# Attention with a feed-forward branch on one core: one PV product cut in two, three PSUM evacuations reordered, and one pair of transfers moved to another queue

## The reference

```python
xn = (x - mean(x)) / sqrt(var(x) + 1e-5)
q, k, v = split_heads(xn @ w_qkv.T + b_qkv)
att = q @ k.T / 4 + bias[head, i - j]          # position bias from cosines and sines
att = softmax(where(causal, att, -inf))
attn = merge_heads(att @ v) @ w_proj.T + b_proj
ffn = bf16(fp8(bf16(xn)) @ fp8(kernel)) + bias_ffn
out = x + attn + ffn
```

## Time and profile before

| | before |
|---|---|
| median of 3 runs | 810.27 us (810.13 to 811.91) |
| profiled execution, its own time | 810.14 us |
| its span, first to last instruction | 808.4 us |
| PE busy | 752.4 us (93%) |
| DVE busy | 624.6 us (77%) |
| ACT busy | 578.6 us (72%) |
| POOL busy | 531.1 us (66%) |
| mean granted TensorE clock | 0.968 |

### The profile page before, as it was taken

How to read it: one execution, slowest core, us unless ns; L and a number is a source line. 1 busy time by engine, 2 the same in 40 slices (tenths; PEclk the granted TensorE clock), 3 DMA queues, 4 the chain that set the end, 5 groups by cost and what they waited for, 6 DMA issues and landing times.

```text
span 808.4 us, 23158 instructions
## 1 busy us (share of the span) xinstructions
PE 752.4 (93%) x6313; PEld 515.3 (64%) x6313; DVE 624.6 (77%) x2395; ACT 578.6 (72%) x1258; POOL 531.1 (66%) x525
## 2 busy tenths in 40 slices
PE   6889999999999999999999999999999999999883
PEld 3556566676666766666676667667676666667552
DVE  3869878887978888787887888798788878888612
ACT  3347868777877868777886777777787777777570
POOL 6435568676666767577666857666676767757570
PEclk8859999999999999999999999999999999999997
DMA  5603333534333253333434243443335334343202
GB/s 172 235 2 140 120 123 114 172 115 151 138 145 136 106 189 119 129 137 145 166 117 149 112 159 112 164 140 145 121 119 179 131 122 138 146 146 114 78 18 86
DMA packets 55612, 106.07 MB, mean 131 GB/s; under 512 B 10528, under 2 KB 30496, under 8 KB 55584
## 3 DMA queue, kind: packets, MB, share of 16 engines
q1 hardware_dynamic: 52680, 102.96, 36.2%
q10 hardware_dynamic: 2904, 2.77, 1.1%
HBM read 18.68 MB, written 8.91 MB: 34 GB/s over the span
## 4 chain that ended last, share of the span: by engine, by line
PE 69%; ACT 7%; DVE 7%; issue 6%; DMA 6%; SPq 3%; ACTq 1%; DVEq 1%; POOL 0%; POOLq 0%
PE misc_a L666 13%; PE misc_a L550 10%; PE misc_b L550 10%; PE scoreT_b L640 8%; PE scoreT_a L640 5%; PE score_a L617 4%; PE score_c L617 4%; DMA x_ring<-in_L_attn_x 4%; PE misc_b L666 3%; SPq L341 3%; ACT probs L925 3%; PE misc_b L601 2%; ACT xnT_hi L821 2%; PE scoreT_c L640 2%; DVE row_max L1003 1%
## 5 line engine op out<-in xcount | busy, mean ns | idle before, releaser
L1201 POOL TENSOR_SCALAR_AFFINE_SELECT probs<-probs 128x512 f32<-128x512 f32 x256 | 161.7, 642 | 231.1 <-ACT probs L925 229.5
L1003 DVE CUSTOM_DVE_ANT_0 score_b<-score_b,causal_mask_q 128x384 f32<-128x384 f32 (+3 forms) x321 | 162.0, 522 | 95.8 <-PE score_b L617 95.6
L1003 DVE CUSTOM_DVE_ANT_0 score_a<-score_a,causal_mask_q 128x512 f32<-128x512 f32 x319 | 174.9, 565 | 6.5 <-PE score_a L617 3.2
L925 ACT ACTIVATE probs<-scoreT_b 128x384 f32<-128x384 f32 (+1 forms) x256 | 134.4, 525 | 63.5 <-PE scoreT_b L640 21.1
L1003 DVE CUSTOM_DVE_ANT_0 score_c<-score_c,causal_mask_q 128x256 f32<-128x256 f32 (+3 forms) x384 | 172.0, 476 | 3.0 <-PE score_c L617 2.8
L925 ACT ACTIVATE probs<-scoreT_a 128x512 f32<-128x512 f32 (+1 forms) x256 | 145.4, 568 | 4.5 <-PE scoreT_a L643 3.7
L1003 DVE DVE_READ_ACCUMULATOR2_ANT row_max<- 128x1 f32 x1024 | 145.6, 142 | 0.0
L925 ACT ACTIVATE probs<-scoreT_c 128x384 f32<-128x384 f32 (+1 forms) x256 | 135.9, 531 | 3.4 <-PE scoreT_c L643 3.0
L666 PE MATMUL misc_a<-probs,v_ones 128*32 128x128 f32 (+3 forms) x1536 | 132.1, 440 | 0.4 <-POOL probs L1201 0.4
L640 PE MATMUL scoreT_b<-stacks 64*128 64x384 f32 (+3 forms) x320 | 120.0, 394 | 5.7 <-ACT probs L925 5.7
L617 PE MATMUL score_b<-stacks 64*128 64x384 f32 (+3 forms) x321 | 118.4, 401 | 1.4 <-DVE row_max L1003 1.4
(11 more groups left out here) (241 smaller groups left out, 1957.3 us busy)
## 6 DMA issues: line engine op xcount, KB each, us to landing
stacks<-qk_parts SPq DMA_DIRECT2D x128, 512.0 KB, 3.9
x_ring<-in_L_attn_x SPq DMA_DIRECT2D x16, 512.0 KB, 3.3
xn<-recips SPq DMA_DIRECT2D x31, 256.0 KB
out<-x_ring SPq DMA_DIRECT2D x15, 512.0 KB, 3.0
attn<-out_T SPq DMA_DIRECT2D x48, 128.0 KB, 2.6
stacks<-neg_max_T SPq DMA_DIRECT2D x128, 4.0 KB
attn<-out_T ACTq DMA_DIRECT2D x16, 128.0 KB, 2.7
low_features<-neg_max_T SPq DMA_DIRECT2D x124, 4.0 KB
```

Source lines behind the costliest of these rows:

```text
L925: A(probs_slot(g, k), STB[(SLOTS * g + k) % 3][:, 0:w], ACT.Exp).then_inc(exp_done, 1)
L1003: last = V.tensor_tensor_reduce(bank, bank, CMQ[:, T - w:T], 1.0, LEAST, ALU.add, ALU.max, MX[:, g % 2, 8 * h + 4 + qt:8 * h + 5 + qt])
L1201: last = GP.affine_select(out=d, in_=d, compare_op=ALU.is_ge, fill=0.0, base=0, pattern=[[0, HU], [1, P]], channel_multiplier=-1)
```

## The change

- Unit 3's PV is cut in two sessions: tile 0 at (0, 0) of the next batch, and tiles 1 to 3 at (0, 3). MT then stands behind the last tile. On ACT, `out_T` comes ahead of `max_T` at (0, 4), and behind it on the others.
- The two transfers of unit 3's result go out on SP's queue, behind `load_max(b, 1)`, and no longer on ACT's (but for the last batch).
- The bf16 copies `XB_evac` wait for `T_lo` and stand at (3, 11) and at (0, 3) of the next batch; they had stood right behind each `XH_evac` at (3, 9) and (3, 10). `T_lo` waits for the high half alone and stands at (3, 9) and (0, 2); it had stood at (3, 10) and (0, 0). The bank of T is free when the bf16 copy is done.
- `invert` moves from (0, 6) to (0, 8). `stats`, `aggregate` and `quant_magic` move to other slots.
- In batch 0 and the setup, the evacuations take the same new order.

```diff
-PV_AT = [(1, 0), (2, 3), (3, 3), (0, 3)]
-PV_REST_AT = {0: (1, 3)}
+PV_AT = [(1, 0), (2, 3), (3, 3), (0, 0)]
+PV_REST_AT = {0: (1, 3), 3: (0, 3)}
...
-XL_AT, FIRST_XL_AT = [(3, 10), (0, 0)], [(0, 3), (0, 3)]
-INVERT_AT, LAST_INVERT_AT = (0, 6), (3, 8)
-STATS_AT, AGGR_AT = [(1, 2), (1, 3), (1, 5), (1, 8)], (1, 9)
-MAGIC_AT = [(2, 0), (2, 1), (2, 2)]
+XB_AT, FIRST_XB_AT = [(3, 11), (0, 3)], (0, 4)
+XL_AT, FIRST_XL_AT = [(3, 9), (0, 2)], [(0, 3), (0, 3)]
+INVERT_AT, LAST_INVERT_AT = (0, 8), (3, 8)
+STATS_AT, AGGR_AT = [(1, 3), (1, 3), (1, 6), (1, 6)], (1, 7)
+MAGIC_AT = [(2, 3), (2, 6), (2, 9)]
...
                 load_max(b, 1)
+                if not first:
+                    regroup(b - 1, 3, False)
...
-                return {"V": (vs_ready, 2 * b + i + 3), "T": (xl_ready, 2 * b + i + 5),
+                return {"V": [(vs_ready, 2 * b + i + 3)], "T": [(xb_ready, 2 * b + i + 5)],
...
-                elif then:
+                elif then and g < 3:
                     job_MT(*then)
...
                 if TT - 1 in tiles:
                     last.then_inc(pv_done, 1)
+                if 0 not in tiles and then and g == 3:
+                    job_MT(*then)
...
             def XB_evac(b, ct):
+                act.wait_ge(xl_ready, 2 * b + ct + 1)
                 A(XB[:, ct, :], misc_of("T", ct)[:, :], ACT.Copy).then_inc(xb_ready, 1)
...
-                if g == 3:
-                    act.wait_ge(ot_ready, 4 * b + 4)
+                if g == 3 and isinstance(b, int) and b == B - 1:
+                    act.wait_ge(ot_ready, 4 * B)
                     send_attn(act, b, 3)
...
                         if k == OUT_AT and not (first and g == 0):
+                            if g == 0:
+                                out_T(pb, pg, False)
                             if not (last and g == 3):
                                 max_T(*((b, g + 1) if g < 3 else (b + 1, 0)))
-                            out_T(pb, pg, first and pg == 0)
+                            if g > 0:
+                                out_T(pb, pg, first and pg == 0)
...
             def T_lo(b, ct):
-                dve.wait_ge(xb_ready, 2 * b + ct + 1)
+                dve.wait_ge(xh_ready, 2 * b + ct + 1)
```

More of the change, by code:

```diff
@@ L528, in _ @@
             mm = nc.tensor.matmul
-            bank_read = [None, None]
+            bank_read = [[], []]
             def done(kind, i, b):
-                return {"V": (vs_ready, 2 * b + i + 3), "T": (xl_ready, 2 * b + i + 5),
-                        "QK": (ql_ready, 4 * b + i + 5), "FF": (y1_ready, 2 * b + i + 1),
-                        "PV": (ot_ready, 4 * b + (i + 1) % G), "PJ": (out_ready, 2 * b + i + 1), "MT": (mts_ready, 4 * b + i + 2)}[kind]
+                return {"V": [(vs_ready, 2 * b + i + 3)], "T": [(xb_ready, 2 * b + i + 5)],
+                        "QK": [(ql_ready, 4 * b + i + 5)], "FF": [(y1_ready, 2 * b + i + 1)],
+                        "PV": [(ot_ready, 4 * b + (i + 1) % G)], "PJ": [(out_ready, 2 * b + i + 1)],
+                        "MT": [(mts_ready, 4 * b + i + 2)]}[kind]
             def misc(kind, i, b):
                 n = MISC_BANK[kind, i]
-                if bank_read[n]:
-                    pe.wait_ge(*bank_read[n])
+                for read in bank_read[n]:
+                    pe.wait_ge(*read)
                 bank_read[n] = done(kind, i, b)
@@ L868, in _ @@
                 XH_evac(0, ct)
+            for ct in range(CT):
                 XB_evac(0, ct)
@@ L930, in body @@
                                 XH_evac(1, i)
-                                XB_evac(1, i)
+                            if first and (g, k) == FIRST_XB_AT:
+                                for i in range(CT):
+                                    XB_evac(1, i)
+                            if (g, k) == XB_AT[1] and not first:
+                                XB_evac(b + 1, 1)
                             for i in due(QK_HI_AT, g, k):
@@ L940, in body @@
                                 XH_evac(b + 2, i)
-                                if i == 0:
-                                    act.wait_ge(xy_ready, b + 1)
-                                XB_evac(b + 2, i)
+                            if (g, k) == XB_AT[0]:
+                                act.wait_ge(xy_ready, b + 1)
+                                XB_evac(b + 2, 0)
                         if not first:
```

## The result

The changed kernel takes 842.25 us (840.23 to 844.54, 4 runs) against 811.09 us (810.13 to 812.26, 4 runs): a ratio of 1.038, interval 1.035 to 1.042. That is slower, as forecast, but by 31 us where 11 were expected, and outside the range. (The table of times further up has three of these four runs of the kernel before.) The profiled execution took 840.23 us with a span of 838.5 us. The granted clock is not the cause: 0.965 over the whole run against 0.968 before, and 1.00 in the steady batch of both.

What follows compares the result with a forecast made beforehand. PE, busy 44.75 of a 46.3 us batch, sets the time. Per batch 1.0 - 0.25 = +0.75 us, 15 times 11.25, less 0.5 in the setup: +10.75, so 821.0 us; range 804.5 to 828.

Steps and rivals of the forecast that it cites:

- part 3: Statistics and rounding on DVE: `quant_magic` in later slots of unit 2 costs 0; moved `stats` wins 0.25 us per batch.
- Part 2: Denominators issued later, on SP, delay DVE's reciprocal; the scores of (1, 0) start 1.0 us late in each batch.
- the faster rival: Denominators are in by 433.55, 0.75 us before the estimate, so nothing is lost: about 804.5 us; chance 0.25.
- the time which ACT wins: ACT drops two issues of 0.56 us each; worth nothing, as PE meets the DVE wait at (1, 0) anyway.
- The rival with the maxima late at (1, 0): Transposed scores of (1, 0) wait for the maxima, half a microsecond more per batch: 828 us; chance 0.05.
- that lateness: Inverses' store and spread some 2.7 us late; POOL uses them some 10 us later, in unit 1: cost 0.
- Part 1: At (0, 2) a 0.63 us exponential wait goes; first PV session waits some 0.8; (0, 4) comes 0.27 late.
- FF's 0.25: Ahead of FF, moving one `stats` wins 0.25 us of PE's 0.4 us wait per batch; bounds 0 and 0.4.
- part 4: Setup: high copies first free most of PE's 0.95 us wait before the first QK; -0.5 us, bounds 0, -0.9.

Runs made afterwards that it cites:

- experiment 1: Changed kernel with the three rounding steps put back at slots 0 to 2 of unit 2: 830.87 us, ratio 1.021 to the kernel before.
- experiment 5: Changed kernel with POOL's bf16 bias addition moved behind the last mask of unit 2, DVE untouched: 830.29 us, ratio 1.021 to the kernel before.
- experiment 6: Kernel before with the rounding steps alone moved to (2, 3), (2, 6) and (2, 9): 823.43 us, ratio 1.014.
- experiment 2: Changed kernel with unit 3's two result transfers ahead of the four maxima transfers on SP: 830.75 us, ratio 1.021 to the kernel before.
- experiment 3: Changed kernel with unit 3's two result transfers back on ACT's queue behind `out_T`: 832.45 us, ratio 1.025 to the kernel before.
- experiment 9: Kernel before with the layer norm's statistics alone moved, as in the change: 808.77 us, ratio 0.997.
- experiment 8: Changed kernel with rounding put back, unit 3's PV in one session, second bf16 copy at (0, 1), its low half at (0, 0): 806.41 us, ratio 0.992.
- experiment 12: Kernel before with SP sending unit 3's result behind the maxima, inversion at (0, 8), and statistics moved: 803.55 us, ratio 0.990.
- experiment 10: Kernel before with unit 3's result sent by SP behind the maxima and the inversion at (0, 8): 806.04 us, ratio 0.993.

## Why the prediction was wrong in size

The direction and its main mechanism held. Its sum was +0.75 us per batch, and +2.0 was measured.

**The step that failed: part 3, "both ways cost 0" for `quant_magic`.** The prediction asked only which slot's slack on DVE the steps would use. It did not ask what POOL does at that moment. Experiments 1, 5 and 6 give the term: +0.75 to +0.77 us per batch, 11 us in all, from a step of 0.69 us stretched to 2.15. The Trainium skill has the rule (SBUF — State Buffer, section "SBUF: two separate sides"): DVE and GpSimd share a pair of ports that is locked for a whole instruction, among others against a DVE instruction with two SBUF inputs, and the one that comes second is blocked. The trace agrees: DVE's instruction ends 0.55 us after POOL's, whether they overlap by 1.6 us or by 0.44. And DVE's result step, with one source in PSUM and one in SBUF, takes its 0.68 us (476.48 to 477.16) within POOL's instruction of 475.10 to 477.48. It is the rule against this change that I should have weighed. The rows for it were in the trace of before: from 402 to 405, where the three steps stood, POOL had instructions on 4 values per partition and a mask; from 405.65 to 408.04 and from 409.79 to 411.94, where they were to go, instructions over 1024 columns.

**Part 2, the way of the denominators: mechanism right, size 1.0 against 1.4.** The links, in us from the batch's start, forecast and found: SP's first maxima transfer 6.64 and 6.80; the denominators' issue 10.09 and 10.56; the reciprocal 12.34 and 12.82; from it to PE's scores 1.31 and 1.23; PE's scores of (1, 0) 13.65 and 14.05, against 12.65 before. From issue to reciprocal it was 2.26 us, where 2.25 was taken. Two links were mis-sized. "The bf16 copy for MT's bank ends a little before that and is hidden behind `out_T`" was wrong: PE waits 0.42 us for it, and `max_T` 0.23 us for MT. And between the fourth maxima issue and the attn issue there were 0.40 us, not 0.13. Experiments 2 and 3 show the cause, by removing the wait in two ways. Four issues again took 2.72 us, and the faster rival, which needed the denominators 0.75 us sooner, falls. That the time which ACT wins is worth nothing against this held: the changed kernel wins 0.4 us from (0, 6) to (0, 9), and loses it again at (1, 0). The rival with the maxima late at (1, 0) came up nowhere. What came up was unit 2's: its four transfers stand behind the spread of the inverses and unit 0's stacks on SP's queue, which the late inversion pushes back, and at (2, 0) PE waited for them in several kernels (in the changed one it comes 0.3 us later from (1, 11) to (2, 0) than before, absorbed by the shorter wait ahead of FF). I had costed that lateness at 0, by looking at POOL's use of the inverses and not at what is queued behind them on SP.

**Part 1: right in its wait, short in its end.** The wait for the first bf16 copy was forecast at 0.8 and found at 0.86 on average (0.81 in this batch); the wait for the exponential went. Slot (0, 4) came 0.73 us late where 0.27 was worked out; the difference is MT's wait, named above, here for PE itself.

**Part 3, FF, and part 4.** FF's 0.25 was found as 0.2 in the changed kernel and 0.2 alone (experiment 9); the setup's 0.5 was found as 0.5.

**The sum with what was measured:** 1.4 - 0.2 + 0.75 = 1.95 per batch, 15 times 29 us, near the measured 31. The range missed for the same reason: the term costed at nothing had no upper bound. Its upper end, +1.2 per batch, is just what the other parts came to (1.4 - 0.2). With 11 us for the missing term, 828 would have been 839; the profiled execution took 840.2, and the median of the four runs lies 2 us above it.

**The wait that was worth little.** In experiment 8 the 0.6 us wait at (0, 2) is gone, in experiment 12 it is still there, and the two kernels are equally fast (45.76 and 45.67 us per batch). PE reaches (0, 2) 1.66 us into the batch in experiment 8, as in the kernel before, because it now waits at (0, 1):

```profile
465.38 0.69 DVE L997 TENSOR_TENSOR xnT_lo<-misc_a,xnT_hi 128x512 fp32r<-128x512 f32 x1
...
466.58 0.14 DVE L1015 DVE_READ_ACCUMULATOR2_ANT row_max<- 128x1 f32 x1
...
466.77 0.49 PE L621 MATMUL score_b<-stacks 64*128 64x512 f32 x1 [0.30 <-DVE row_max L1015]
```

The low half of T now stands on DVE ahead of the maxima of (3, 10), which that slot needs. And in the kernel before, the maxima that (0, 2) needs were there only at 423.78, and its plain scores started at 423.86:

```profile
423.64 0.14 DVE L1003 DVE_READ_ACCUMULATOR2_ANT row_max<- 128x1 f32 x1
...
423.86 0.49 PE L617 MATMUL score_c<-stacks 64*128 64x512 f32 x1
```

Two limits stood at one place, and PE's list of waits names one of them. What experiment 8 wins, it wins where experiment 12 does, at (0, 7) to (0, 9) and ahead of FF.

**What stays open.** These are readings of the timelines; no run moved DVE's low half alone.

## What to carry to other kernels

An instruction is not moved only against its own engine's slack: look at what the engine that shares its memory ports runs at the new place, and price the overlap at the whole length of that instruction. A transfer moved to another queue is late by every issue ahead of it (0.68 us each here), makes everything behind it late too, and is harmless only if the queue's head leaves soon enough, which another part of the same change may prevent. A change of several tables should be taken apart before it is judged: this one held two parts worth 1% together, under a net loss of 31 us.

## What the runs showed of the hardware

- A DVE instruction with two SBUF sources of 128 x 512 takes 0.69 us alone, 0.99 where POOL's 128 x 1024 instruction still ran for its first 0.4, and 2.15 where it began 0.53 us behind one of 2.13 us. In both cases it ends 0.55 us after POOL's. The result step on DVE, with one source in PSUM and one in SBUF, took 0.68 to 0.69 us in both kernels, beside such an instruction of POOL or not.
- Four small transfers took 2.72 us to issue on SP's queue in most places, but 3.73 where they came right behind two transfers of the stacks. From SP's queue in the changed kernel:

```profile
452.87 1.21 SPq L378 DMA_DIRECT2D stacks<-qk_parts  x2
454.21 3.73 SPq L342 DMA_DIRECT2D stacks<-neg_max_T  x4
```

The same four took 3.57 us in experiment 10 and 3.84 in experiment 2. In the kernel before, where 1.5 us lay between them, it was 2.76.
